# Graph attention on one core: VectorE adds a unit's sums one step earlier (lag 26 in place of 27)

## What is computed

```
xl = (x @ W_l).reshape(n, H, C)
xr = (x @ W_r).reshape(n, H, C)
feat = xl[src] + xr[dst]
feat = where(feat >= 0, feat, 0.2 * feat)
logits = einsum('ehc,hc->eh', feat, att)
ex = exp(logits - segment_max(logits, dst)[dst])
alpha = ex / (segment_sum(ex, dst)[dst] + 1e-16)
out = segment_sum(alpha[:, :, None] * xl[src], dst)
```

## Time and profile before

| | |
|---|---|
| runs timed | 3 |
| median | 2596.53 us |
| lowest, highest | 2594.55, 2596.93 us |
| span of the profiled execution, first to last instruction | 2585.0 us |
| median of the runs less that span | 11.5 us |
| TensorE busy, share of the span | 2017.0 us, 78% |
| VectorE busy | 1562.0 us, 60% |
| GpSimd busy | 1338.7 us, 52% |
| ScalarE busy | 1265.0 us, 49% |

### The profile page before, as it was taken

One profiled execution on the slowest core, in us unless ns is written; L12 is line 12 of the kernel. 1 busy time (PEld: TensorE's weight loads), 2 busy tenths in 40 slices (PEclk: granted clock), 3 DMA queues, 4 the chain that ended last, 5 costly groups with the idle time before them and its releaser, 6 DMA issues. The chain is left out here.

```text
span 2585.0 us, 44303 instructions
## 1 busy us (share of the span) xinstructions
PE 2017.0 (78%) x9489; PEld 1658.9 (64%) x9490; DVE 1562.0 (60%) x3500; ACT 1265.0 (49%) x3196; POOL 1338.7 (52%) x1263
## 2 busy tenths in 40 slices
PE   3965888888888888888788888873876519999994
PEld 2754666666666666666666666652766518888884
DVE  6955777777777777777777777789455510111110
ACT  2542666556666556566566656652545402322331
POOL 3346566656666566665666666619004452444442
PEclk9987899889999899999999999985885559999997
DMA  7676666666666666666666666625502345666665
GB/s 212 235 246 181 191 189 193 179 179 195 185 186 187 182 186 192 190 185 190 185 184 187 191 186 183 188 60 170 164 16 96 116 129 155 146 138 144 142 146 140
DMA packets 255242, 436.15 MB, mean 169 GB/s; under 512 B 41849, under 2 KB 126754, under 8 KB 255062
## 3 DMA queue, kind: packets, MB, share of 16 engines
q1 hardware_dynamic: 156320, 234.21, 29.8%
q0 software_dynamic: 66272, 154.09, 24.3%
q10 hardware_dynamic: 32598, 47.26, 5.8%
HBM read 370.08 MB, written 71.74 MB: 171 GB/s over the span
## 5 line engine op out<-in xcount | busy, mean ns | idle before, releaser
L816 POOL DMA_INDIRECT ring<-xl_rows,a_idx x928 | 931.0, 1003 | 589.1 <-issue 250.6
L1161 PE MATMUL a_o_ps<-ring,a_hot_e 128*128 128x264 f32 x1856 | 531.8, 413 | 190.1 <-DVE acc L1036 141.2
L1148 PE MATMUL a_f_ps<-a_xr_w,a_hot_n 128*128 128x268 f32 x1856 | 586.4, 399 | 44.0 <-ACT a_lg L904 20.7
L1150 PE MATMUL a_f_ps<-ring,ident 128*128 128x264 f32 x1856 | 603.9, 409 | 0.0
L1006 DVE SCALAR_TENSOR_TENSOR a_pos<-a_f_ps,att_ext 128x528 f32<-128x528 f32 x464 | 324.9, 700 | 370.8 <-PE a_f_ps L1150 171.6
L1161 PEld LDWEIGHTS a_o_ps<-ring,a_hot_e 128*128 128x128 f32 x1856 | 354.6, 200 | 298.5 <-issue 218.0
L1148 PEld LDWEIGHTS a_f_ps<-a_xr_w,a_hot_n 128*128 128x128 f32 x1856 | 368.6, 203 | 119.0 <-issue 52.2
L904 ACT COPY a_lg<-a_f_ps 128x8 f32<-128x8 f32 x464 | 79.7, 172 | 518.0 <-DVE a_pos L1006 383.6
L1016 DVE TENSOR_REDUCE a_lg<-a_pos 128x8 f32<-128x528 f32 x464 | 322.7, 695 | 2.1 <-issue 1.3
L1024 DVE TENSOR_TENSOR ring<-ring (+1 forms) x464 | 315.9, 681 | 0.1
L1974 POOL DMA_INDIRECT acc_rows<-ring,x_idx x112 | 175.4, 1566 | 261.8 <-DVE ring L2072 146.0
(11 more groups left out here) (318 smaller groups left out, 2178.9 us busy)
## 6 DMA issues: line engine op xcount, KB each, us to landing
a_xr_w<-xr_rows SPq DMA_DIRECT2D x464, 268.0 KB
a_rel_bc<-rel_rows ACTq DMA_DIRECT2D x116, 256.0 KB
x_w<-in_L_ffn_W_dram SPq DMA_DIRECT2D x56, 512.0 KB
ring<-xl_rows,a_idx POOLq DMA_INDIRECT x928
ring<-disp_rows SPq DMA_DIRECT2D x56, 257.0 KB
xr_rows<-xr_parts SPq DMA_DIRECT2D x50, 268.0 KB, 2.1
xl_rows<-xl_sb SPq DMA_DIRECT2D x50, 132.0 KB, 2.0
j_xl<-xl_rows SPq DMA_DIRECT2D x25, 264.0 KB, 2.9
```

The source lines that it names most:

```text
L816: nc.gpsimd.indirect_dma_start(xl_e[:, p * T + 2 * h + u, :], None, k.xl_rows, bass.IndirectOffsetOnAxis(ap=idx[:, p, 2 * h + u:2 * h + u ...
L1148: nc.tensor.matmul(f_ps[:, g, u, 0:XRW], hot_n[:, j % 2, 2 * g + u, :], xr_w[:, h % XR, a, :].bitcast(F32R), start=(a == 0), stop=False)
L1150: last = nc.tensor.matmul(f_ps[:, g, u, 0:XW], k.ident[:, :], xl_e[:, p * T + 2 * h + u, :], start=False, stop=True)
L1161: last = nc.tensor.matmul(o_ps[:, hh % 2, 0:XW], hot_e[:, j % 2, 2 * g + u, :], xl_e[:, pp * T + 2 * hh + u, :], start=(u == 0), stop=(u = ...
```

## The change

One constant changes. It moves L1036 in VectorE's stream, and the table of blocks with it; TensorE's lag `SUM = 26` stays. So VectorE adds in step n the sums that TensorE makes in its step n, and no longer those of step n-1.

```
-ADD = 27
+ADD = 26
```

## The result

The changed kernel took 2610.89 us (median of 13 runs, 2592.34 to 2635.87) against 2596.53 us for the kernel before (13 runs, 2588.43 to 2605.93). The ratio of the runs is 1.0053, 95% interval 1.0033 to 1.0073: +14 us (9 to 19). The forecast was 2628 us, +32. The sign was right and the size more than twice too large. A second comparison of the same two kernels, on another chip, gave 1.0092 (1.0056 to 1.0127), +24 us; the two intervals overlap between about 15 and 19 us.

What follows compares the result with a forecast made beforehand. Neither TensorE nor VectorE is full; their waits for each other in the attention were taken as the bound. Chunk start 18 + late signals 26 - freed wait 12 = +32 us, 2617, plus 11.5 outside the span: 2628 us, range 2564 to 2668.

Steps and rivals of the forecast that it cites:

- The ring of two engines: Attention: VectorE waits for TensorE's logits ahead of L1006 (299 us), TensorE for VectorE's add ahead of L1161 (141.2 us).
- the sign: Whole kernel: the change makes it slower, +32 us; slower by over 0.2% was given 0.62.
- The signs that I named in the profile: L1161's wait near zero, new L1036 wait 100 to 250 us, less idle ahead of L1006, h = 1 later by 0.6 us.
- I take half of that, 12 us: TensorE's freed wait for the add ahead of L1161: VectorE uses half of 25 us, so -12 us.
- The chunk start, 18 us; nothing covers it: At h = 0 transposes delay the sums, so VectorE's add waits: 28 chunk starts, 0.64 us each, +18 us.
- 32 times the sum alone is late, 26 us: VectorE's add waits for late sum signals in 32 steps: 51 us at most, half taken, +26 us.
- A: Rival, attention: TensorE's freed wait wins, with less time at the lower clock; 2565 us, faster; chance 22%.
- B: Rival, attention: one wait replaces another and the chunk-start price is taken up; 2596 us, within 5 us; chance 12%.
- C: Rival, attention: lockstep, VectorE becomes the bound, each step with an add pays 0.22 us; 2710 us; chance 5%.

Runs made afterwards that it cites:

- w_all: Kernel before, lag 27 kept, VectorE also waiting ahead of each add for the sum TensorE makes in the same step; 1.0156, +40 us.
- b3_27: Kernel before, lag 27 kept, with three PSUM places for the sums instead of two; 0.9900, on a second chip 0.9902.
- w_start: Kernel before, lag 27 kept, VectorE's added wait for the same step's sum only at h = 0; 1.0006, on other chips 0.9995, 0.9976, 0.9988.
- w_rest: Kernel before, lag 27 kept, VectorE's added wait for the same step's sum only at h != 0; 1.0162, on other chips 1.0112, 1.0136.
- add2_26_2: Lag 26 with VectorE's add between L1024 and L1016, against the kernel before, on a slower chip; 0.9956, -11 us.
- add3_27: Kernel before, lag 27 kept, with the add last in VectorE's step, on the quick chip; 1.0151, +34 us.
- add2_26: Lag 26 with VectorE's add between L1024 and L1016, against the kernel before; 1.0051, +12 us on the quick chip; repeated on a slower one, 0.9956.

## Why the prediction was off, step by step

**The ring of two engines and the sign: right.** VectorE's new wait costs (+40 us in w_all) and TensorE's freed wait gives (-26 us in b3_27). That their difference is the first comparison's +14 us is in part luck: on the second chip the terms give +2 and the change +24. The signs that I named in the profile came: L1161's wait for L1036 near zero, 100 to 250 us ahead of L1036 (124), less idle time ahead of L1006. L1006 of h = 1 was to come 0.6 us later against that of h = 0; by my count over n = 32 to 432 it came 1.4 us later (mean distance 4.28 us before, 5.70 after). The two waits of VectorE together were to be over 305 us; by the rows above they are 121.4 + 97.0 + 124.3 = 343 us.

**"I take half of that, 12 us": wrong, the term that was mis-sized first.** The freed wait is worth 26 us, twice measured with three places. My own number before the halving was 25: 70 us, of which VectorE uses the share of steps in which it stands idle. That the two agree is no proof of the 25, which held nothing for the clock, and the clock rose in b3_27. I halved it on the strength of one step in which VectorE had a backlog; that backlog itself came from a wait of 2.25 us for TensorE's logits, in the first of these rows. With three places TensorE's wait for the add falls to 21 us, and VectorE's two waits for logits from 299 to 261 us:

```profile
DVE a_pos L1009 <- remote: 133.1, 58, 5.7
DVE a_pos L1009 <- PE a_f_ps L1153: 127.8, 67, 4.8
...
PE a_o_ps L1164 <- DVE acc L1039: 20.9, 21, 2.9
```

**"The chunk start, 18 us; nothing covers it": wrong.** The mechanism is there and even dearer than I read it. In the changed kernel, at step n = 400:

```profile
1512.89 0.71 DVE L1006 SCALAR_TENSOR_TENSOR a_pos<-a_f_ps,att_ext 128x528 f32<-128x528 f32 x1
1513.07 0.68 PE L1174 MATMUL a_sm_ps<-ident,a_lg 128*128 128x128 f32 x2 [3.69 <-DVE a_lg L1016]
1513.54 1.97 PE L1161 MATMUL a_o_ps<-ring,a_hot_e 128*128 128x264 f32 x4
...
1515.75 0.43 DVE L1036 TENSOR_TENSOR acc<-a_o_ps,acc 128x264 f32 x1 [2.15 <-PE a_o_ps L1161]
```

TensorE has idled 3.69 us for the reduce, runs its sums in 1.97 us where the earlier trace rows have 1.13 (the granted clock there is 0.50, the 1.2 GHz level, as after the stall of the earlier trace rows), and VectorE waits 2.15 us. 17 of the 27 chunk starts from n = 32 on have this wait of 2.1 to 2.2 us. But before the change VectorE idled at the same steps ahead of L1006: by my count 70 us at h = 0, against 15 us ahead of L1006 and 48 us ahead of L1036 after it. In w_start it is 34 and 31 us. So the wait moved by one instruction, and w_start costs nothing, on four of the slower chips. I had looked at two chunk starts, 240 and 272, and 272, which gave the upper price, is one without that idle time; the sum over all of them was to be had from the trace of before.

**"32 times the sum alone is late, 26 us": too small.** The wait in the other steps cost 29 to 42 us in w_rest, some of which can be TensorE's added waits for the add. The count was the difference of two engines' numbers of waits, a weak stand-in: w_rest has 83 adds that wait more than 1 us. The three corrections, -18 at the chunk start, +9 here (with w_rest's mean) and -14 for the freed wait, take the forecast from +32 to +9 us. The two comparisons measured +14 (9 to 19) and +24 (15 to 33), so the corrected sum fits the first at its edge and not the second.

**Rivals.** A needed the freed wait at its full worth and a higher clock. With three places both came (0.902 against 0.891 and 0.884, whole execution); in the changed kernel the clock did not rise (0.94 in both windows). B, within 5 us of no change, and C, 2710 us, are out by the result itself, 2610.89 us.

**Settled and open.** Shown: the chunk start costs nothing on the slower chips, the wait in the other steps costs, the freed wait is worth twice my 12 us with three places, and lag 26 is faster than the kernel before when the add stands last. Argued only: that the price of the wait lies in long waits for late signals. For it are the trace of w_rest, in which they hold 140 of the 182 us, and the quick chip, where such waits are missing; against it is add2_26_2, and w_rest was never run on the quick chip. What holds TensorE's signals back for microseconds on most chips isn't known: the profile names no releaser. Open as well is why the terms don't add up to the change on the second chip.

**A better version.** Lag 27 with three PSUM places beats both kernels: 0.9900 and 0.9902, 26 us below the one before on two chips. Lag 26 with the add last and three places does as well on another (0.9905).

## What to carry to other kernels

A lag between two engines sets two waits at once, the consumer's for data and the producer's for a free buffer; measure each by itself (a wait for a later count; one more buffer) together with the change on the same chip, and see whether they add up, which they did not here. In this kernel one more buffer was the better trade. At lag 26 it also paid to put the instruction that needs the freshest data last in its step, behind those that others wait for; at lag 27, on the quick chip, the same place cost 34 us. Before pricing a wait at a recurring place, add up over all its occurrences what idle time already stands just ahead of it; two examples misled me here.

## What the hardware showed that I had not expected

One kernel takes 2266 us on one chip and 2560 to 2598 us on five others, each within about 1% of itself. The difference is in the attention: VectorE's instructions last the same, and TensorE's do at the full clock (0.386 us is the median of its L1161 in both). But between 270 and 1740 us of the trace of before, 120 of 439 L1006 start more than 0.3 us, up to 5.8 us, after both VectorE is free and the modelled end of the logits, 267 us in all by my count, and in the trace of add3_27 none does. TensorE's clock differs too: its mean from the first logits to the last add is 0.93 in before and 1.00 in add3_27. The kernel before was not profiled on the quick chip, so this sets two kernels against each other. And a change can have opposite signs on the two kinds: add2_26 is 0.44% faster on one (0.9956, 0.9935 to 0.9978) and 0.51% slower on the other (1.0051, 1.0038 to 1.0064).
